# Causal mask of the transposed scores: zeros set by GpSimd after the exponentials instead of a mask product on TensorE

## What is computed

```python
scores = jnp.einsum('bhqd,bhkd->bhqk', q, k)
causal = jnp.tril(jnp.ones((S, S), dtype=bool))
scores = jnp.where(causal, scores, -jnp.inf)
probs = jax.nn.softmax(scores, axis=-1)
attn = jnp.einsum('bhqk,bhkd->bhqd', probs, v)
```

## Time and profile before

| | us |
|---|---|
| median of 3 runs | 757.46 |
| lowest and highest | 755.2, 760.0 |
| the profiled execution | 756.01 |
| its span, first to last instruction | 754.2 |

### The profile page before, as it was taken

One profiled execution on the slowest core, in us unless ns is written; L12 is line 12 of the kernel. 1 busy time (PEld: TensorE's weight loads), 2 busy tenths in 40 slices (PEclk: granted clock), 3 DMA queues, 4 the chain that ended last, 5 costly groups with the idle time before them and its releaser, 6 DMA issues.

```text
span 754.2 us, 11132 instructions
## 1 busy us (share of the span) xinstructions
PE 585.8 (78%) x3698; PEld 418.1 (55%) x3698; DVE 539.3 (72%) x1129; ACT 319.8 (42%) x581; POOL 263.1 (35%) x242
## 2 busy tenths in 40 slices
PE   3933567977665878999577998898887869999990
PEld 2721345645442666888434565455454458888880
DVE  5868997978779665776396876886886157777753
ACT  2376533323110212345304664454454546666640
POOL 3147476835456653427565001001004401211210
PEclk9975669989777889999757999999998999999996
DMA  5101200000011200075999563442001696000005
GB/s 185 54 31 56 80 2 0 1 1 0 0 29 53 58 27 1 1 178 127 177 264 125 69 79 57 68 58 31 2 2 58 233 421 256 27 24 29 30 22 181
DMA packets 43623, 58.39 MB, mean 77 GB/s; under 512 B 7184, under 2 KB 37072, under 8 KB 42544
## 3 DMA queue, kind: packets, MB, share of 16 engines
q1 hardware_dynamic: 41696, 52.55, 29.6%
q0 software_dynamic: 1872, 5.13, 1.9%
HBM read 41.97 MB, written 15.51 MB: 76 GB/s over the span
## 4 chain that ended last, share of the span: by engine, by line
PE 36%; DVE 11%; DMA 3%; issue 2%; ACT 2%; POOL 1%; SPq 0%; ACTq 0%; POOLq 0%; DVEq 0%
PE bank L750 17%; DVE small L1701 5%; PE bank L997 4%; PE bank L974 4%; PE bank L947 4%; PE bank L744 4%; DMA pieces<-P 2%; PE bank L949 1%; PE bank L976 1%; DMA yt<-results 1%; POOL P L2135 1%; DVE mtok L1712 1%; PE bank L1014 1%; ACT PTa L1273 1%; DVE XA L1730 0%
## 5 line engine op out<-in xcount | busy, mean ns | idle before, releaser
L1701 DVE TENSOR_REDUCE small<-bank 128x1 f32<-128x256 f32 (+3 forms) x256 | 107.3, 482 | 10.4 <-PE bank L949 9.5
L2040 POOL TENSOR_TENSOR al<-hm,ah 128x512 fp32r<-128x512 f32 (+1 forms) x28 | 40.9, 1462 | 92.8 <-ACT ah L1236 89.8
L947 PE MATMUL bank<-Ks,Qs 96*128 96x256 bf16 (+3 forms) x256 | 67.2, 330 | 5.3 <-DVE small L1701 3.7
L1979 DVE TENSOR_TENSOR wl<-wall,wh 128x1024 fp32r<-128x1024 f32 x46 | 56.1, 1221 | 19.8 <-ACT wh L1387 19.8
L974 PE MATMUL bank<-Qs,Ks 99*128 99x512 bf16 (+3 forms) x256 | 59.1, 308 | 4.9 <-issue 4.5
L1273 ACT ACTIVATE PTa<-bank 128x512 f32<-128x512 f32 (+1 forms) x96 | 43.6, 528 | 29.9 <-PE bank L976 29.6
L1273 ACT ACTIVATE PTb<-bank 128x512 f32<-128x512 f32 (+1 forms) x96 | 43.7, 529 | 28.2 <-PE bank L976 27.8
L949 PE MATMUL bank<-maskb,identb 128*128 128x128 bf16 x256 | 55.6, 236 | 0.0
L1572 DVE TENSOR_TENSOR_SCAN S<-AT,U 128x512 f32<-128x512 f32 x32 | 49.2, 1537 | 8.8 <-POOL QS L2058 8.5
L974 PEld LDWEIGHTS bank<-Qs,Ks 99*128 99x128 bf16 x256 | 25.4, 99 | 46.9 <-issue 29.9
L750 PE MATMUL bank<-XTh,wgu 128*128 128x512 f32 x64 | 35.6, 556 | 20.2 <-DVE hm L1526 20.2
(11 more groups left out here) (351 smaller groups left out, 1640.7 us busy)
## 6 DMA issues: line engine op xcount, KB each, us to landing
wall<-e_pack SPq DMA_DIRECT2D x8, 1536.0 KB, 12.1
pieces<-P SPq DMA_DIRECT2D x12, 512.0 KB, 10.1
Qs<-pieces SPq DMA_DIRECT2D x48, 128.0 KB, 5.4
Ks<-pieces SPq DMA_DIRECT2D x48, 128.0 KB, 6.1
stg<-w_pack SPq DMA_DIRECT2D x18, 256.0 KB, 2.7
wf<-t_pack SPq DMA_DIRECT2D x12, 256.0 KB, 2.7
sorted_rows<-blank SPq DMA_DIRECT2D x1, 2944.0 KB, 13.1
yt<-results SPq DMA_DIRECT2D x8, 256.0 KB, 4.2
```

The costliest lines, as they stand in the source:

```text
L947: nc.tensor.matmul(banks[b][:, o:o + w], Q[0:96, h, i * P:(i + 1) * P], K[0:96, h, 0:w], start=True, stop=False)
L1701: last = nc.vector.tensor_reduce(mxv[:, i, h:h + 1], banks[b][:, o:o + w], AX.X, ALU.max, negate=True)
L1979: nc.vector.tensor_tensor(flat(moe["wl"][:, i % 2, half]), wall[:, bass.ds(place + half * KC * EI, KC * EI)], flat(moe["wh"][:, i % 2, hal ...
L2040: nc.gpsimd.tensor_tensor(al[0:M, s % 3, :], hm[0:M, s % 3, :], ah[0:M, s % 3, :].bitcast(F32), ALU.subtract).then_inc(*alr.tick(s))
```

## The change

The mask products of the transposed scores (line 976) go. Instead GpSimd gets a share of step `("st", g)`: when all three pieces of head g's exponentials are done, two `affine_select` instructions set zeros where the key is later than the query, in place: one on the diagonal blocks of key tiles 0, 1 and 2 (3 x 128 elements per partition, at 0, 512 and 1024), one on that of tile 3 (128 elements, at 896). A new tally `below` counts them, and `attend` waits for the two of the quad's last head instead of for its exponentials. The scores by query keep their mask product, so the maxima are unchanged.

```diff
+        below = tally("probabilities_masked")
...
+        PT_AT = [0, 512, 1024, 896]
...
-                        nc.tensor.matmul(banks[b][:, o:o + w], K[0:99, h, j * P:(j + 1) * P], Q[0:99, h, j * P:CH],
-                                         start=True, stop=False)
-                        last = nc.tensor.matmul(banks[b][:, o:o + P], maskb[:], identb[:], start=False, stop=True)
+                        last = nc.tensor.matmul(banks[b][:, o:o + w], K[0:99, h, j * P:(j + 1) * P], Q[0:99, h, j * P:CH],
+                                                start=True, stop=True)
...
-                    for i_ in range(3):
-                        pe.wait_ge(*ex.upto((4 * q + 3, i_)))
+                    for i_ in range(2):
+                        pe.wait_ge(*below.upto((4 * q + 3, i_)))
...
+                elif op == "st":
+
+                    g = it[1]
+                    pt = L1["PTa" if g // 4 % 2 == 0 else "PTb"][:, g % 4, :]
+                    pool.wait_ge(*ex.upto((g, 2)))
+                    v = pt.rearrange("p (b n) -> p b n", n=2 * P)[:, 0:5:2, 0:P]
+                    nc.gpsimd.affine_select(v, v, [[0, 3], [1, P]], ALU.is_ge, 0.0, base=0, channel_multiplier=-1)\
+                        .then_inc(*below.tick((g, 0)))
+                    v = pt[:, PT_AT[3]:PT_AT[3] + P]
+                    nc.gpsimd.affine_select(v, v, [[1, P]], ALU.is_ge, 0.0, base=0, channel_multiplier=-1)\
+                        .then_inc(*below.tick((g, 1)))
```

More of the change, by code:

```diff
@@ L973, in scores_t @@
                         w = (4 - j) * P
-                        nc.tensor.matmul(banks[b][:, o:o + w], K[0:99, h, j * P:(j + 1) * P], Q[0:99, h, j * P:CH],
-                                         start=True, stop=False)
-                        last = nc.tensor.matmul(banks[b][:, o:o + P], maskb[:], identb[:], start=False, stop=True)
+                        last = nc.tensor.matmul(banks[b][:, o:o + w], K[0:99, h, j * P:(j + 1) * P], Q[0:99, h, j * P:CH],
+                                                start=True, stop=True)
                         o += w
                     last.then_inc(*mm.tick(("st", g, i_)))
-            PT_AT = [0, 512, 1024, 896]
             def attend(q, j):
```

## The result

The changed kernel takes 762.5 us (median of 8 runs, 759.2 to 763.9) against 757.9 (8 runs, 755.2 to 760.4) for the kernel before on the same chip: ratio 1.0058, 95% interval 1.0038 to 1.0078, or 4.4 us more. The forecast was 767.0, 9.5 us more, and a loss of over 1% as the likeliest; it is a loss of 0.6%, inside the range of 757 to 780. The chip matters: on a second one, where the kernel before takes 767.3 us, the change costs nothing (0.9991, interval 0.9967 to 1.0014). So I first read where the 5.65 us between the two profiled spans (754.2 and 759.9) lie, then why the chips differ.

The account below looks back on a forecast made before the run. TensorE was taken to bound most of the attention stage, VectorE some stretches; -7.8 (removal) + 6.3 (VectorE held up) + 11.0 (tail) = +9.5 us, giving 767.0 us from a median of 757.5, range 757 to 780.

Parts of the forecast that it names:

- The removal: Attention stage before 568 us: dropping four mask products a head gains 7.8 us where TensorE is the bound.
- 34 x 0.23: 34 heads in TensorE-bound stretches before 568 us, each gaining 0.23 us from four masks: 7.8 us.
- The selects' rate: On GpSimd, a head's two selects take 1.1 us, between 0.82 and 1.48.
- rival 1: Hardly any loss: selects at the one-input rate (0.82 us), no meeting with VectorE, 758.7 us; chance 0.32.
- VectorE held up: Selects on GpSimd delay VectorE's small operations on SBUF, not its reduces: 6.3 us in the attention stage.
- 8 x 0.5 = 4.0: In about 8 quads of TensorE-bound stretches, VectorE's waiting and its closeness to TensorE's pace cost 0.5 us each.
- 15 selects at 0.15: In the stretches bound by VectorE, some 15 selects cost 0.15 us each, 2.3 us together.
- Net ahead of the slots: Before the routed rows' slots: 7.8 us gained by the removal against 6.3 us lost on VectorE.
- The tail: End of attention stage: selects queued around GpSimd's indirect DMAs make quad 15's product 11 us late; 9 at 0.82 a pair.
- both idles of TensorE: Behind 568 us TensorE idles 4 us or more twice, the second time ahead of quad 14's product until a select ends.
- the second group's queue: Selects of heads 56 to 59 stand behind the second eight indirect DMAs; quad 14's product comes 9.4 us late.
- head 53's wait: First eight indirect DMAs stand behind head 53's select, begin 6.6 us later; TensorE's line 959 comes 4.5 us late.

Follow-up runs that it names:

- e4: Kernel before without any causal mask of the transposed scores, neither product nor select, on all 64 heads; second kind of chip: ratio 0.9904.
- e6: Kernel before with no mask of the transposed scores on heads 0 to 51, product from 52 on, no selects; second kind of chip: ratio 0.9883.
- e3: Kernel before, product kept on all heads, with selects added on heads 0 to 51; second kind of chip: ratio 1.0032.
- e1: Changed kernel with selects only on heads 0 to 51, product from 52 on; second kind of chip: ratio 0.9932 to the kernel before.
- e10: Changed kernel with selects only on heads 0 to 51, product from 52 on; first kind of chip: ratio 0.9957 to the kernel before.
- r1: The kernel before, unchanged, traced on the second kind of chip: ratio 0.9998, tail 41.6 us.
- late stores: Kernel before with the second group of stores issued only behind head 63's exponentials; run twice, first kind of chip: ratios 1.0116 and 1.0120.
- e9: Changed kernel, but heads 53 to 55 keep the product and have no select; first kind of chip: ratio 1.0049 to the kernel before.

## Why the prediction was right or wrong

- **The removal, 7.8 us: 1.5 us too much.** By the slots, the two kernels with no mask ahead of them (e4, e6) stand at 160.1 on average, the six with the product at 166.4: 6.3 us. The step that failed is "34 x 0.23": in the TensorE-bound stretch three heads of a quad gave 0.24 us each and the first head nothing, since ScalarE's exponentials hold it up: 0.69 a quad, not 0.92. Quads 1 to 4 gave 2.8 us of the 3.7 counted for them, the rest up to the slots 3.5 of 4.1, with quad 7 slower at its lower clock. By total time e6 gave 9.0, more than its trace's marks explain.
- **The selects' rate, 1.1 us a pair: 0.72 back to back, 0.82 by durations.** A one-input rate, as rival 1 had it. (The Trainium skill, GPSIMD Engine Reference, § 7, gives 1.03 to 2.03 cycles an element at 1.2 GHz. From 128 to 384 elements a select grows by 228 ns, 0.89 ns or 1.07 cycles an element: the low end.)
- **VectorE held up, 6.3 us: the step that failed most.** "8 x 0.5 = 4.0" and 15 selects at 0.15 took a meeting as likely. The traces show 6 meetings and 1.6 us. The mechanism is right; the waiting itself is a quarter of the term. By time, the selects cost 2.5 to 3.8 us on 52 heads (e3, and e1 against e6), about half of it. Where the part over 1.6 us lies is not shown, and e3's interval (1.2 to 3.7) takes in 1.6.
- **Net ahead of the slots: -1.5 forecast, -3.75 in the pair of traces**, -3.1 as the mean of seven traces with selects against six with the product.
- **The tail, 11 us: 9.24, and 9 was the forecast's own figure for a pair at 0.82.** Stores 6.2 us later (6.6 forecast), the copy 3.6 us (4.5), and both idles of TensorE are there, 5.23 and 1.39 us. The second was to be 4 us or more: TensorE was late itself, from the first wait and the cold clock behind it. Quad 14's product came 7.2 us late (9.4 forecast), and the way from there to quad 15's took 2.1 us longer (1.5 forecast). What was wrong is the weight: I called the second group's queue the largest term. Taken away alone it gives 1.4 us, head 53's wait taken away alone 3.5. The rest, 4.3 us, comes back whichever of them goes. Half of it is the 2.1 us between quad 14's product and quad 15's, which stand in all four traces with selects there on this kind of chip (8.9 to 9.1 us, where it was 7.0). Two parts of these show: quad 14's first products at the lower clock (1.05 us before, 1.7 to 1.9 with selects) and the wait for head 63's select (0.81 before, 1.65 with it). For the other 2.2 us one wait takes the place of the other. No run took both away, so how these divide stays open.
- **The sum.** -3.75 + 9.24 and the two small differences of the table make 5.65 by the spans, 4.4 by the medians' ratio, between rival 1 (+1.2) and the forecast (+9.5). So the path was right and the sizes off: the forecast failed by the 6.3 us, of which 2.5 to 3.8 came, and by the tail's 11, of which 9.24 came; the 7.8 us, of which 6.3 came, hid a part of both. The chance of 0.62 on a loss of over 1% rested on the 6.3 us and on the same tail on every chip.
- **Not foreseen at all:** on two of five chips the kernel before has its own tail stretched, so that the change is even there.

What beats both kernels is e10: selects as far as head 51, the product from 52 on, ratios 0.9957 and 0.9932 on the two kinds of chip, both intervals below 1.

## What to carry to other kernels

Work moved to an idle engine is free only where nothing urgent is queued there: this change won 3 to 4 us in the long stretch and, on the first kind of chip, lost 9 on the dozen heads around the idle engine's one urgent job, so move such work by condition. When two waits stand in one chain, price each by what is left when it alone is gone, since the next one takes its place. A shared lock is priced by how often two instructions meet (here 6 of some 125), not by the length of one.

## What the runs showed of the hardware

- **A stretch of the tail that depends on the chip.** On three of five chips ScalarE runs heads 53 to 60 as soon as their scores are there; on two, in eight kernels of eight, it starts an instruction near each group of indirect stores 2.5 to 5 us late. Near the second group this is always head 58, 2.3 to 2.7 us behind the last store's start; in r1 that was 595.62 and 598.27. The cause is open: moving with the stores speaks for them, always head 58 for the program, and the first group fits neither strictly. The run that was to tell them apart (late stores) twice fell on a chip without the stall.
- **The same instructions can meet another granted clock, and then take longer.** e9 and e10 run the same up to head 52, and one quad took 19.6 us at a granted clock of 0.75 to 0.83, 15.1 at 0.99 to 1.00. The unchanged kernel took 15.3 us for it at 1.00 in one trace and 16.7 at 0.90 in another (r1). What sets the fall off in one execution and not in the other is not shown.
- **A select with a strided view** over three blocks of 128 costs 522 ns, no more than a plain one-input operation on 384 elements (517).
